# A two-layer decoder kernel in f32: attention units of half a batch, split 128x64 scores, and new orders in two stages

## The reference

```
ch_bias = (max(xp, rows) + min(xp, rows)) / 2
xz      = xp - ch_bias
idx     = number of thresholds tmax / 2^k below the channel's cmax
scale   = tmax / 2^(7 - idx) / 7
result  = clip(round(xz / scale), -8, 7) * scale
y       = result @ W_quantised.T + ch_bias @ W.T + b
```

## Time and profile before

| | us |
|---|---|
| median of 3 runs | 3158.14 |
| lowest and highest | 3135.93 and 3161.92 |
| the profiled execution | 3147.52 |
| its span, first to last instruction | 3145.4 |

### The profile page before, as it was taken

How to read it: one execution, slowest core, us unless ns; L and a number is a source line. 1 busy time by engine, 2 the same in 40 slices (tenths; PEclk the granted TensorE clock), 3 DMA queues, 4 the chain that set the end, 5 groups by cost and what they waited for, 6 DMA issues and landing times. The chain is left out here.

```text
span 3145.4 us, 62447 instructions
## 1 busy us (share of the span) xinstructions
PE 2807.8 (89%) x22416; PEld 2429.2 (77%) x22416; DVE 1988.1 (63%) x4026; ACT 1320.8 (42%) x3154; POOL 1278.0 (41%) x1605
## 2 busy tenths in 40 slices
PE   6999999995899999999999699967999999599994
PEld 6999999994788888888888688855777777477773
DVE  5555555554788888888888544434667665366666
ACT  2222222223666666666566422212333322166666
POOL 3111111112576766667676211112454444234444
PEclk9999999997999999999999899986889877699996
DMA  3000000002000000000000100010000000010001
GB/s 132 7 7 7 3 7 7 7 0 91 6 3 5 3 5 3 5 4 4 5 3 3 41 0 0 0 32 11 8 7 10 7 7 4 23 35 27 27 11 58
DMA packets 42646, 49.08 MB, mean 16 GB/s; under 512 B 4176, under 2 KB 33744, under 8 KB 42064
## 3 DMA queue, kind: packets, MB, share of 16 engines
q1 hardware_dynamic: 42576, 48.16, 4.6%
HBM read 35.57 MB, written 4.19 MB: 13 GB/s over the span
## 5 line engine op out<-in xcount | busy, mean ns | idle before, releaser
L1077 POOL TENSOR_TENSOR b_rows<-b_rows,b_swapped 128x512 f32<-128x512 f32 x160 | 204.1, 1284 | 133.4 <-DVE b_swapped L864 133.4
L1018 ACT ACTIVATE b_probs<-bank,b_shift,b_q_scale 128x128 f32<-128x128 f32 x512 | 227.8, 458 | 71.1 <-DVE b_shift L895 71.0
L504 POOL TENSOR_TENSOR a_probs<-a_probs,a_rs 128x512 f32<-128x512 f32 x64 | 66.8, 1044 | 324.3 <-DVE a_rs L403 317.1
L46 PE MATMUL bank<-a_xT,a_wq 128*128 128x256 f32 x512 | 153.8, 300 | 39.8 <-DVE a_xT L370 39.8
L1124 POOL TENSOR_TENSOR b_probs<-b_probs,b_rs 128x512 f32<-128x512 f32 x128 | 133.2, 1040 | 111.3 <-DVE b_rs L915 108.0
L2577 ACT ACTIVATE d_probs<-d_probs 128x512 f32<-128x512 f32 x128 | 78.5, 629 | 229.0 <-DVE d_probs L2474 229.0
L1087 POOL TENSOR_TENSOR b_rms<-b_rms,sh_minus_half 128x8 f32<-128x8 f32 (+1 forms) x128 | 169.6, 1325 | 10.6
L872 DVE TENSOR_REDUCE b_ss<-b_squares 128x4 f32<-128x512 f32 x192 | 125.2, 680 | 61.0 <-ACT b_squares L993 61.0
L46 PE MATMUL bank<-b_wo,b_oT 128*128 128x256 f32 x512 | 150.7, 294 | 1.4 <-DVE b_oT L838 1.4
L47 PE MATMUL bank<-a_xT,a_wq 128*128 128x256 f32 x512 | 148.7, 290 | 0.0
L48 PE MATMUL bank<-a_xT,a_wq 128*128 128x256 f32 x512 | 148.3, 290 | 0.0
(11 more groups left out here) (347 smaller groups left out, 9432.6 us busy)
## 6 DMA issues: line engine op xcount, KB each, us to landing
a_xT_in<-in_xT SPq DMA_DIRECT2D x16, 256.0 KB, 2.5
sh_x<-in_x SPq DMA_DIRECT2D x1, 4096.0 KB, 25.0
b_ctx_in<-in_ctxT SPq DMA_DIRECT2D x32, 128.0 KB, 2.0
d_x_in<-sh_x SPq DMA_DIRECT2D x16, 256.0 KB, 2.3
e_x_in<-sh_x SPq DMA_DIRECT2D x16, 256.0 KB, 2.3
e_cT<-in_ctxT SPq DMA_DIRECT2D x32, 128.0 KB, 2.5
out<-sh_x SPq DMA_DIRECT2D x16, 256.0 KB, 2.1
a_qT<-in_L_attn_Wq SPq DMA_DIRECT2D x1, 2048.0 KB, 8.5
```

The lines of the kernel that those rows point to most:

```text
L46: pe.matmul(out, left[0], right[0], start=start, stop=False)
L1018: op = act.activation(probs[:, g % 2, keys], bS[:, keys], ACT.Exp, bias=shift[:, g % 2, a:a + 1], scale=q_scale[:, g, a // 2, a % 2:a % 2 ...
L1077: pool.tensor_tensor(rows[:, unit, :], rows[:, unit, :], swapped[:, half, :], ALU.add).then_inc(added[unit], 1)
```

## The change

Self-attention: each score product of two heads (128 columns of weights) becomes two products of one head (64 columns), on the two halves of the partitions:

```diff
-last = pe.matmul(bS[:, o:o + S], qT[:, g, 2 * r + b, 2 * p:2 * p + 2, :].rearrange("p h q -> p (h q)"),
-                 kT[:, g, (2 * r + b) * S:(2 * r + b + 1) * S], start=True, stop=True)
+for h in range(2):
+    last = pe.matmul(bS[h * S:(h + 1) * S, o:o + S], qT[:, g, 2 * r + b, 2 * p + h, :],
+                     kT[:, g, (2 * r + b) * S:(2 * r + b + 1) * S], start=True, stop=True)
```

```diff
+b = 2 * r + half
 for c in range(C):
     for n in range(4):
-        rows = slice(32 * n, 32 * n + 32)
-        for b in range(2):
-            op = pe.matmul(bS[n][b * S:(b + 1) * S, c * 256:(c + 1) * 256],
-                           qT[rows, i.k, c, (2 * r + b) * S:(2 * r + b + 1) * S],
-                           keys[rows, i.k, c, 2 * r + b].rearrange("p h k -> p (h k)"), start=True, stop=True)
-op.then_inc(scored[r], 1)
+        rows, side = slice(32 * n, 32 * n + 32), n % 2
+        op = pe.matmul(bS[2 * half + n // 2][side * S:(side + 1) * S, c * 256:(c + 1) * 256], qT[rows, i.k, c, b * S:(b + 1) * S],
+                       keys[rows, i.k, c, b].rearrange("p h k -> p (h k)"), start=True, stop=True)
+op.then_inc(scored[b], 1)
...
-        j = 8 * c + 2 * n + p
-        for b in range(2):
-            op = pe.matmul(bO[b * S:(b + 1) * S, j * VW:(j + 1) * VW], pT[:, u % 2, 2 * c + p, b * S:(b + 1) * S],
-                           v[:, i.k, 2 * r + b, j // 2, :], start=True, stop=True)
+        slot = 4 * n + 2 * c + p
+        for side in range(2):
+            j = 8 * c + 2 * (2 * (n % 2) + side) + p
+            op = pe.matmul(bO[side * S:(side + 1) * S, slot * VW:(slot + 1) * VW], pT[:, u % 2, 2 * c + p, side * S:(side + 1) * S],
+                           v[:, i.k, u // 2, j // 2, :], start=True, stop=True)
 op.then_inc(weighed[u], 1)
```

PE, DVE and ACT of the grouped stage get new orders; `maximum` waits for the call that serves its own batch (`scored[u // 2]`), `residual` also for the normalising of the block before, and POOL adds the bias for `mid`, not `old`:

```diff
 def turn(new, mid, old, oldest):
-    project_v(mid)
-    turn_probs(old, 0, 7, True)
-    weigh(oldest, 7)
-    scores(old, 1, 1, False)
-    turn_probs(old, 1, 0, False)
-    turn_att(oldest, mid)
-    weigh(old, 0)
-    turn_probs(old, 2, 1, False)
+    project_out(oldest, mid)
+    turn_probs(old, 3, 2, False)
     turn_x(new, oldest)
-    weigh(old, 1)
-    turn_probs(old, 3, 2, False)
-    project_out(oldest, mid)
+    weigh(old, 2)
     turn_probs(old, 4, 3, False)
-    weigh(old, 2)
     weigh(old, 3)
-    scores(mid, 0, 6, True)
+    scores(mid, 0, 1, 7, True)
     turn_probs(old, 5, 4, False)
+    project_k(new)
     weigh(old, 4)
     turn_probs(old, 6, 5, False)
-    project_k(new)
+    scores(mid, 1, 0, 1, False)
     weigh(old, 5)
-    project_q(new, oldest)
     turn_probs(old, 7, 6, False)
     weigh(old, 6)
+    project_q(new, oldest)
+    weigh(old, 7)
+    scores(mid, 1, 1, 2, False)
+    turn_probs(mid, 0, 7, True)
+    project_v(new)
+    turn_probs(mid, 1, 0, False)
+    turn_att(old, new)
+    weigh(mid, 0)
+    turn_probs(mid, 2, 1, False)
+    weigh(mid, 1)
+    scores(new, 0, 0, 5, True)
...
 def turn(new, mid, old, oldest):
+    residual(oldest)
+    maximum(mid, 5)
+    shift(mid, 3)
+    shift(mid, 2)
+    maximum(mid, 4)
     moments(oldest)
     take_att(old, 1, 7)
     maximum(mid, 7)
-    maximum(mid, 5)
-    maximum(mid, 4)
     shift(mid, 4)
     shift(mid, 5)
     maximum(mid, 6)
+    shift(mid, 6)
+    maximum(new, 0)
     shift(mid, 7)
-    shift(mid, 6)
-    residual(old)
+    shift(new, 0)
+    maximum(new, 1)
     take_att(mid, 0, 3)
+    maximum(new, 2)
+    shift(new, 1)
     maximum(new, 3)
-    maximum(new, 2)
-    maximum(new, 0)
-    maximum(new, 1)
-    shift(new, 0)
-    shift(new, 3)
-    shift(new, 2)
-    shift(new, 1)
...
 def turn(new, mid, old, oldest):
-    exponent(old, 3)
-    take_pT(old, 2, 0, False)
-    exponent(old, 4)
+    take_pT(old, 4, 2, False)
     take_x(new)
-    take_pT(old, 3, 1, False)
-    exponent(old, 5)
-    take_pT(old, 4, 2, False)
-    exponent(old, 6)
+    exponent(old, 7)
+    exponent(mid, 0)
     take_pT(old, 5, 3, False)
+    exponent(mid, 1)
+    take_pT(old, 6, 4, False)
+    take_pT(old, 7, 5, False)
     take_k(new)
-    exponent(old, 7)
-    take_pT(old, 6, 4, False)
     take_q(new)
-    exponent(mid, 0)
-    take_pT(old, 7, 5, False)
-    exponent(mid, 1)
     exponent(mid, 2)
     take_pT(mid, 0, 6, True)
-    take_v(new, old)
+    exponent(mid, 3)
     take_pT(mid, 1, 7, True)
     take_att(old)
+    take_v(new, old)
+    take_pT(mid, 2, 0, False)
+    exponent(mid, 4)
+    exponent(mid, 5)
+    take_pT(mid, 3, 1, False)
+    exponent(mid, 6)
```

Quantised stage: `project_k`, `project_q`, `project_v` and `project_out` are split in halves of four instructions (`o` or `r` = 0 and 1; all semaphores at the same ends), `take_v` likewise; `project_q` waits for the restored x too. The value bias no longer goes into `qc.spread`: a one-time product with the out weights goes into `out_bias`, which PE and POOL wait for before the loop:

```diff
+pe.wait_ge(w_loaded, 16 * N_LOADS)
+for c in range(C):
+    op = pe.matmul(bP[:, 0:D], b_cols[:, V, c:c + 1].to_broadcast([128, 128]), w[:, O, c, :], start=(c == 0), stop=(c == C - 1))
+op.then_inc(v_bias_through, 1)
...
 dve.wait_ge(w_loaded, 16 * N_LOADS)
+dve.wait_ge(v_bias_through, 1)
+dve.tensor_tensor(out_bias[:, :], bP[:, 0:D], b_out[:, :], ALU.add).then_inc(out_bias_ready, 1)
...
-def spread_bias(i):
-    if i is None:
-        return
-    pool.wait_ge(qx.bias_ready, this(i))
-    pool.wait_ge(v_ready, last(i))
+def spread_bias(i, q, used):
+    if i is None:
+        return
+    pool.wait_ge(q.bias_ready, this(i))
+    pool.wait_ge(used, last(i))
     hold(pool, sh.passed_pool)
-    pool.tensor_copy(qx.by_chunk(qx.spread[:, :, :]), qx.over_rows(qx.bias[:, :])).then_inc(qx.spread_ready, 1)
-def spread_ctx_bias(i):
-    if i is None:
-        return
-    pool.wait_ge(qc.bias_ready, this(i))
-    pool.wait_ge(y_ready, last(i))
-    pool.tensor_tensor(qc.spread[:, :, :].rearrange("p c (m r) -> p c m r", r=CHUNK),
-                       qc.bias[:, :].rearrange("p (c m) -> p c m", c=C).unsqueeze(3).to_broadcast([128, C, M, CHUNK]),
-                       b_cols[:, V, :].unsqueeze(2).unsqueeze(3).to_broadcast([128, C, M, CHUNK]), ALU.add).then_inc(qc.spread_ready, 1)
+    pool.tensor_copy(q.by_chunk(q.spread[:, :, :]), q.over_rows(q.bias[:, :])).then_inc(q.spread_ready, 1)
```

`add_out_bias` then adds `out_bias` in place of `b_out`. The orders of PE, DVE, ACT and POOL in the quantised stage:

```diff
 def turn(new, mid, old, oldest):
-    weigh(old, 4)
-    project_k(mid, oldest)
-    project_q(mid)
+    scores(mid, 0, 0, 5, True)
     weigh(old, 7)
-    project_out(oldest, mid)
-    scores(mid, 0, 0, 5, True)
     turn_x(new, oldest)
-    project_v(mid)
+    project_v(mid, 1)
+    weigh(old, 6)
     scores(mid, 0, 1, 7, True)
     scores(mid, 1, 0, 1, False)
     turn_probs(mid, 0, 7, True)
     turn_att(old, mid)
     weigh(mid, 0)
     turn_probs(mid, 1, 0, False)
-    scores(mid, 1, 1, 2, False)
+    scores(mid, 1, 1, 3, False)
     turn_probs(mid, 2, 1, False)
-    turn_cmax(new, qx, bX[1], qc, old, v_taken)
     weigh(mid, 1)
+    weigh(mid, 2)
+    turn_cmax(new, qx, bX[1], qc, old, v_taken[1])
     turn_probs(mid, 3, 2, False)
     spread_x(new)
+    turn_probs(mid, 4, 3, False)
+    turn_cmax(old, qc, bX[0], qx, new, res_ready)
     weigh(mid, 3)
-    turn_probs(mid, 4, 3, False)
-    weigh(mid, 2)
-    turn_cmax(old, qc, bX[0], qx, new, res_ready)
     turn_probs(mid, 5, 4, False)
     spread_att(old)
+    weigh(mid, 5)
     turn_probs(mid, 6, 5, False)
-    weigh(mid, 5)
-    weigh(mid, 6)
+    project_k(new, old, 0)
+    project_k(new, old, 1)
+    project_q(new, 0)
+    weigh(mid, 4)
+    project_q(new, 1)
     turn_probs(mid, 7, 6, False)
+    project_out(old, new, 0)
+    project_out(old, new, 1)
+    project_v(new, 0)
 pe.wait_ge(w_ready, 4)
-pe.wait_ge(w_loaded, 16 * N_LOADS)
+pe.wait_ge(out_bias_ready, 1)
 pe.wait_ge(zeroed, 3)
 four_deep(pe, n_turns, turn)
...
 def turn(new, mid, old, oldest):
-    moments(oldest)
-    maximum(mid, 0)
-    maximum(mid, 1)
-    shift(mid, 0)
+    shift(mid, 1)
     lowest(new, qx, bX[0])
-    shift(mid, 1)
     highest(new, qx, bX[0])
+    take_att(old, 1, 6)
+    maximum(mid, 2)
     maximum(mid, 3)
-    maximum(mid, 2)
+    shift(mid, 2)
+    widest(new, qx)
     shift(mid, 3)
-    widest(new, qx)
+    lowest(old, qc, bX[1])
     highest(old, qc, bX[1])
-    lowest(old, qc, bX[1])
-    shift(mid, 2)
-    maximum(mid, 5)
+    centre(new, qx, bX[0])
+    maximum(mid, 4)
     centre(old, qc, bX[1])
-    maximum(mid, 4)
-    widest(old, qc)
     shift(mid, 4)
     find_top(new, qx, bX[1])
-    centre(new, qx, bX[0])
-    maximum(mid, 6)
+    maximum(mid, 5)
+    widest(old, qc)
     shift(mid, 5)
     thresholds(new, qx, bX[1])
+    maximum(mid, 6)
+    maximum(mid, 7)
     shift(mid, 6)
-    maximum(mid, 7)
+    count(new, qx)
+    add_bias(new)
     find_top(old, qc, bX[0])
-    count(new, qx)
-    take_att(mid, 0, 2)
-    shift(mid, 7)
+    take_att(mid, 0, 3)
     invert(new, qx)
     thresholds(old, qc, bX[0])
     divide(new, qx)
     restore(new, qx, v_ready)
     count(old, qc)
+    shift(mid, 7)
     invert(old, qc)
-    add_bias(new)
     divide(old, qc)
+    restore(old, qc, y_ready)
     take_k(new)
-    restore(old, qc, y_ready)
-    take_att(mid, 1, 7)
     take_q(new)
     residual(old)
+    moments(old)
+    maximum(new, 0)
+    maximum(new, 1)
+    shift(new, 0)
...
 def turn(new, mid, old, oldest):
-    take_pT(mid, 0)
+    exponent(mid, 2)
+    take_pT(mid, 1)
     exponent(mid, 3)
-    exponent(mid, 1)
```

(23 more changed lines are left out.)

147 lines of the change are left out of this document (82 added, 65 removed).

## The result

The changed kernel takes 3125.7 us (median of 6 runs, 3123.1 to 3128.8) against 3152.0 for the kernel before (3135.9 to 3161.9) on the same chip: ratio 0.9921, interval 0.9893 to 0.9949. I had forecast 3163, on a median of 3158 from the first three runs of the kernel before: a little slower, and it came out faster. The profiled execution took 3125.2 us, its span is 3123.2.

A forecast was written before the change was run, and what follows sets the result against it. PE was taken to be busy most of the span, its clock down mainly in the quantised stage. Terms -8 + 17 - 5 + 1.5 = +5.5 us on a median of 3158.1 gave 3163 us, range 3115 to 3215.

The forecast's parts named there:

- Self-attention, -8: Self-attention: scores as 128x64 make a call 0.53 us shorter; fifteen turns at 0.53 give -8 us.
- only call 3 of 4: Self-attention: of calls 0 to 3 in a turn, only the last gains its whole 0.53 us; others gain 0.1 at most.
- Grouped stage, +17: Grouped stage: two more score calls of about 1.0 us make a turn 20.3 for 19.23 us, +17 us in all.
- Row groups that share a bank: Rival, grouped and quantised stages: row groups writing one bank serialise, a call lasts 0.86 us longer; 3245 us, chance 0.08.
- Quantised stage, -5: Quantised stage: a turn averages 34.4 for 34.7 us, minus 0.3 a turn times 16, -5 us.
- the shares of those 14 turns: Quantised stage: new turn prices of 31.5, 33, 34.6 and 37 us, weighted by the old clock shares, average 34.4.
- The price at full clock (31.5): Quantised stage: a full-clock turn takes 31.5 us, +1.8, with out projection and half of v ending last.
- the once-only product: Ahead of the quantised stage's loop: product with the value bias and the waits for it, +1.5 us (0 to 3).
- The longer pair of calls: Quantised stage: two score calls now on the same tiles take +0.7 us, where DVE has other work; no direct cost.
- Keeps its clock: Rival, quantised stage: full clock, 31.5 us in all turns; total 3121 us, chance 0.18.
- Slow in the dense tail: Rival, quantised stage: clock falls just ahead of key, query, out and value projections; turn 37, total 3203 us, chance 0.20.

The follow-up runs named there:

- e13: Kernel before with each of the two score calls of a grouped-stage turn done twice over, same results: 3163.5 us, ratio 1.0042.
- e6: Like e4, with nine products of no use added to each quantised-stage turn, in its later half: 3116.2 us, ratio 0.9892.
- e5: Like e4, but the quantised stage keeps the units of before; its orders, projection halves and once-only value bias are new: 3123.4 us, ratio 0.9925.
- e4: The changed kernel with the grouped stage of before: 3106.0 us, ratio 0.9862.
- e9: Like e5, with two products of no use a turn ahead of the attention's transposes in the quantised stage: 3108.6 us, ratio 0.9848.
- e15: Like e1, with the second of the four score calls of a quantised-stage turn done twice over: 3208.8 us, ratio 1.0186.
- e14: Like e1, with two products of no use a turn ahead of the attention's transposes in the quantised stage: 3118.6 us, ratio 0.9900.
- e10: Kernel before with 128x64 self-attention scores and, in the quantised stage, new units of half a batch in the old orders: 3102.8 us, ratio 0.9836.
- e11: Like e10, with two products of no use added to each quantised-stage turn: 3118.7 us, ratio 0.9894.
- e12: Like e11, with two more products a turn, four in all: 3122.4 us, ratio 0.9896.
- e17: Like e10, with seven products of no use added to each quantised-stage turn: 3098.7 us, ratio 0.9856.
- e1: Kernel before with the changed 128x64 scores of self-attention alone: 3140.5 us, ratio 0.9952.

## Why the prediction was wrong

- **Self-attention, -8.** The mechanism and the term were right: 0.57 us a turn for the forecast 0.53, only call 3 of 4, the rest turned into waits (a_xT from 39.8 to 49.5 us, a_probs from 0.4 to 17.9). Missed: some 6 us for four turns at clock 0.96 that no longer occur, and some 3 at the ends of the stage.
- **Grouped stage, +17.** Right: turn 20.51 for 20.3, stage +19.1, the waits of the earlier trace rows gone, PE the bound; e13 bears out the passes. That calls of 16 instructions last 1.09 us was right too.
- **Row groups that share a bank** do not take turns: 1.09 us with two row groups on the two halves of one bank, the same as the earlier trace rows. The Trainium skill, "TensorEngine Tiling (Array Packing)", Gotcha 1, would forbid such a pair. The Trainium skill, "PSUM — Partial Sum Buffer", section "PSUM bank collisions raise a hardware error", quotes the same rule, but what it reports as measured between two row tiles is a collision in the same bank and the same quadrant. Here the two row groups write different quadrants at the full rate, and the measurement decides.
- **Quantised stage, -5: the step that failed** is the line "with the shares of those 14 turns (3 turns full, 2 near 0.9, 5 at 0.81, 4 about 0.70)". I priced a turn at each clock and kept the shares of before, as if the clock were given from outside. But the shares are made by the kernel. Of the 14 turns none stayed at 0.70 and none at 1.00; ten ran at 0.85, three at 0.89 and one at 0.79. They average 33.33 us, not 34.4, which is 15 us in all. My own prices, read between their points at the clocks measured, give 33.8 (an estimate), so some 8 of the 15 us are the shares and some 7 are prices that were too high: 0.2 us at 0.85, 0.8 at 0.89, 2 at 0.79. The price at full clock (31.5) agrees with the 31.2 to 31.5 estimated from e6.
- **The stage's ends.** From the last transposing of x to its end the stage takes 84.0 us for 91.0; I had given that stretch 0.3. Its head, with the once-only product, is 0.4 us longer for the +1.5 forecast.
- **The longer pair of calls.** The forecast wrote it off: "+0.7 us, but at a place where DVE has other work, so it costs nothing directly". It costs nothing, and the units that bring it are the larger part of the stage's gain (0.9925 in e5, 0.9862 in e4; e9, with two products in their place, 0.9848). PE's idle time there goes from 1.07 to 0.51 us. I had looked for costs only.
- **Rivals.** "Keeps its clock" came nearest in size (3121), for another reason: the clock rose from 0.79 to 0.83, while no turn was at full clock. "Slow in the dense tail" happened in part: the clock does fall ahead of the key projection (2421.6 for 2426.41), but it is back at 2431.8, ahead of the out projection and the half of v. In e15 its price and more (40.6 a turn, clock 0.71) was paid, for a wait elsewhere.
- **Sum by what was measured:** -17.9 + 2.9 - 26.3 + 19.1 = -22.2 on the profiled executions (3147.5 to 3125.2), and 26 on the medians. Six microseconds of the 37 between 3163 and 3126 are the median of the kernel before, 3158 when I forecast and 3152 over six runs.

**What stays open:** why the filled gap gives all of the units' gain in the new orders and less than half in the old. e14 leaves a wait of 0.68 us behind the gap where e10 has 0.42, which points to the handover, but no run changed that wait alone. A rival stands beside it: that every small edit draws its own mixture of turns, as e11 and e12 did. It fits e14 and e15 too. Against it speak e9, which runs through e4's cycle, and e17, which met its forecast. That the turns of self-attention lost their slow spells through the shorter calls is seen in every profile with them; no run looked for the reason.

## What to carry to other kernels

When PE's granted clock moves between turns of the same loop, price a change twice: what it does to a turn at each clock, and what it does to PE's idle gaps, since here the slow turns came and went with them. Work added in a gap can be a gain (e9), and can be a loss (e11, e12). Half a microsecond of new wait went with 5 us more a turn. A gain of this kind is fragile: repeat it over several runs, and test each part alone, as here the new orders of the quantised stage gave 0.3%, within the intervals, and the change of the grouped stage took 19 us.

## What the runs showed of the hardware

- One program, ten runs (e1): 3122 us at mean clock 0.938, 3146 at 0.927. The changed kernel (six runs) and e4 (four) spread over 6 us only; their turns repeat a fixed cycle (33.4, 33.6, 33.9, 32.3).
- In the changed kernel's turns of the quantised stage, from the third on, the clock is at 1.2 GHz for one stretch of 7 to 10 us that begins 13.3 to 15.0 us into the turn. In the kernel before the stretch is missing in three turns and 24 us long in four.
- A score call on four tiles takes 1.09 us for 16 instructions, on eight tiles 1.12 for 32: passes on one tile follow at 0.21 us, whatever the others do. 64-column f32 loads on alternating sides let 32 products pass in 1.15 us where 16 of 128 columns took 1.90.
- In e15 a wait 0.57 us longer stands beside a clock of 0.71 over the 15 turns where e1 has 0.83, and 580 us where e1 has 501 in the fastest of its ten runs.
